# Six instead of four buffers for the down-projection weights, and a later softmax epilogue, in a fused attention and FFN kernel

## The reference

```python
xn = _layernorm(x, axis=-1)
latent = xn @ Wc_down                                  # 1024 -> 512
q = (latent @ Wq_up).reshape(Bsz, Tlen, N_HEAD, HEAD_DIM)
kv = latent @ Wkv_up; k, v = kv[..., :64], kv[..., 64:]
att = softmax(causal(einsum('bthd,bsd->bhts', q, k) * scale))
s = einsum('bhts,bsd->bthd', att, v).reshape(Bsz, Tlen, C) @ Wc_proj
h = _silu(xn @ (w_gate/127).T) * (xn @ (w_up/127).T)
g = _silu(h @ (w_down/127).T)
out = x + s * g
```

## Time and profile before

| | us |
|---|---|
| median of 2 runs | 3336.55 (3332.39 to 3340.7) |
| the profiled execution | 3337.86 |
| its span, slowest core (core 1) | 3336.1 |
| spans of the 8 cores | 3316.5 to 3336.1 |
| mean granted TensorE clock, core 1 | 0.808 |
| ACT busy, core 1 | 1308.0 |
| DVE busy, core 1 | 1181.9 |

### The profile page before, as it was taken

The page is one execution under the profiler, slowest core; times in us unless marked ns, Lnnn a source line. Parts: engine busy times, 40 slices in busy tenths (PEclk is TensorE's granted clock), DMA queues, the critical chain, the costliest instruction groups (busy, mean ns, idle before and its releaser), DMA issues.

```text
span 3336.1 us, 33293 instructions; the slowest of 8 cores (3316.5 to 3336.1 us)
## 1 busy us (share of the span) xinstructions
PE 2123.8 (64%) x10464; PEld 995.9 (30%) x10464; DVE 1181.9 (35%) x1978; ACT 1308.0 (39%) x1457; POOL 417.1 (13%) x329
## 2 busy tenths in 40 slices
PE   2324545466565674785758758587575887587876
PEld 1112323222331341442225222252231442223421
DVE  4635443432533435424243251422322422511221
ACT  0112232312321332433634436344455437376365
POOL 0211221223133011101101001100111001011011
PEclk9556767767787796897879968799788899699997
DMA  5031346759476153351015300153001250011510
GB/s 92 28 65 41 51 79 81 112 92 147 57 87 111 47 123 112 73 137 43 27 46 121 102 15 26 40 134 96 13 20 40 62 147 30 22 27 39 146 39 14
DMA packets 547288, 232.14 MB, mean 70 GB/s; under 512 B 476464, under 2 KB 532784, under 8 KB 547120
## 3 DMA queue, kind: packets, MB, share of 16 engines
q1 hardware_dynamic: 429792, 186.88, 21.5%
q0 software_dynamic: 117328, 43.14, 12.1%
HBM read 241.62 MB, written 27.26 MB: 81 GB/s over the span
## 4 chain that ended last, share of the span: by engine, by line
PE 39%; DVE 20%; DMA 15%; ACT 10%; issue 10%; POOL 4%; DVEq 1%; SPq 0%; ACTq 0%; POOLq 0%
PE ps_sc L566 9%; PE ps_y L553 9%; ACT p_sb L577 9%; PE ps_u L724 5%; PE ps_u L731 4%; POOL p_sb L585 4%; DVE recbf L605 3%; PE ps_u L795 3%; DMA wd_t<-wdbf 3%; DMA wu_t<-wu 3%; DMA xt<-xb 3%; DMA wd_t<-wd 2%; PE ps_u L643 2%; DVE stat L303 2%; DVE xnT L377 2%
## 5 line engine op out<-in xcount | busy, mean ns | idle before, releaser
L577 ACT ACTIVATE p_sb<-ps_sc 128x1024 bf16<-128x1024 f32 x1088 | 1089.1, 1024 | 1460.3 <-PE ps_sc L566 1453.6
L553 PE MATMUL ps_y<-p_sb,vaug_sb 128*65 128x512 bf16 x2176 | 747.4, 429 | 245.6 <-POOL p_sb L585 143.6
L566 PE MATMUL ps_sc<-qs,kT_sb 65*128 65x512 bf16 x2176 | 745.9, 428 | 26.7 <-DVE qs L534 26.7
L585 POOL TENSOR_TENSOR p_sb<-p_sb,masks_sb 128x1024 bf16<-128x1024 bf16 x128 | 277.5, 2177 | 2361.0 <-ACT p_sb L577 2360.7
L553 PEld LDWEIGHTS ps_y<-p_sb,vaug_sb 128*65 128x65 bf16 x2176 | 214.6, 120 | 682.3 <-issue 607.3
L370 PE MATMUL ps_u<-ident_sb,xn_t 128*128 128x128 bf16 x512 | 65.5, 271 | 413.3 <-DVE xn_t L333 236.2
L795 PE MATMUL ps_u<-wd_t,h_sb 128*128 128x512 bf16 x768 | 219.8, 415 | 154.4 <-DMA wd_t<-wd 59.1
L566 PEld LDWEIGHTS ps_sc<-qs,kT_sb 65*128 65x128 bf16 x2176 | 222.0, 107 | 242.8 <-issue 103.1
L724 PE MATMUL ps_u<-xnT_own,wg_t 128*128 128x256 bf16 x1536 | 224.0, 294 | 83.9 <-DVE h_sb L742 60.1
L595 DVE CAST yf<-ps_y 64x1024 bf16<-64x1024 f32 x32 | 38.8, 1213 | 591.3 <-PE ps_y L553 591.3
L731 PE MATMUL ps_u<-xnT_own,wu_t 128*128 128x256 bf16 x1536 | 218.4, 290 | 15.0 <-DMA wu_t<-wu 14.9
(11 more groups left out here) (85 smaller groups left out, 1249.3 us busy)
## 6 DMA issues: line engine op xcount, KB each, us to landing
wg_t<-wgbf SPq DMA_DIRECT2D x144, 256.0 KB, 3.4
wu_t<-wubf SPq DMA_DIRECT2D x144, 256.0 KB, 3.8
wd_t<-wdbf SPq DMA_DIRECT2D x288, 128.0 KB, 2.2
xt<-xb SPq DMA_DIRECT2D x64, 512.0 KB, 4.5
wg_t<-wg POOLq DMA_DIRECT2D x48, 256.0 KB, 7.7
wu_t<-wu POOLq DMA_DIRECT2D x48, 256.0 KB, 8.7
wd_t<-wd POOLq DMA_DIRECT2D x96, 128.0 KB, 4.2
xo_t<-xo SPq DMA_DIRECT2D x16, 512.0 KB, 4.1
```

The source lines that it names most:

```text
L553: last = O("tensor", lambda e_, t=t, nh=nh, par=par: e_.matmul(ps_y[0:65, nh * 512:(nh + 1) * 512], vaug_sb[:, t, :], p_sb[:, par, nh * 51 ...
L566: sct = O("tensor", lambda e_, t=t, nh=nh, sb2=sb2: e_.matmul(ps_sc[:, sb2 * 1024 + nh * 512:sb2 * 1024 + (nh + 1) * 512], kT_sb[0:65, t * ...
L577: ex = O("scalar", lambda e_, sb2=sb2: e_.activation(p_sb[:, sb2, :], ps_sc[:, sb2 * 1024:(sb2 + 1) * 1024], AF.Exp), [sct, st["p_war"][sb ...
L585: mtoks[t] = O("gpsimd", lambda e_, pview=pview, mj=mj: e_.tensor_tensor(pview, pview, masks_sb[:, mj, :].unsqueeze(1).broadcast_to([128, ...
```

## The change

It has two parts. The ring of `wd_t` gets six buffers in place of four, with the loads issued six tiles ahead; six is also the number of tiles in one step. EPI_DELAY goes from 6 to 10 ticks. The write-backs keep their four chains of semaphores (`wb{seq % 4}`).

```diff
--- before.py
+++ after.py
@@ -154,7 +154,7 @@
     wproj_sb = sbuf("wproj_sb", [128, DK, D], BF16)
     wg_t = sbuf("wg_t", [128, 3, DK, 128], BF16)
     wu_t = sbuf("wu_t", [128, 3, DK, 128], BF16)
-    wd_t = sbuf("wd_t", [128, 4, 512], BF16)
+    wd_t = sbuf("wd_t", [128, 6, 512], BF16)
     ident_sb = sbuf("ident_sb", [128, 128], BF16)
     ident2_sb = sbuf("ident2_sb", [128, HD], BF16)
     masks_sb = sbuf("masks_sb", [128, 4, 128], BF16)
@@ -262,7 +262,7 @@
             "xnacc": [None, None],
             "xnT_war": None, "p_war": [None, None], "yT_war": [None, None],
             "o_war": [None, None], "qs_war": None, "hbuf_war": t_teff,
-            "wg_war": [None, None, None], "wu_war": [None, None, None], "wd_war": [None] * 4,
+            "wg_war": [None, None, None], "wu_war": [None, None, None], "wd_war": [None] * 6,
             "vt_war": t_consts, "scbf_war": None, "latq_war": None,
             "ytmp_war": (), "yf_war": None, "rec_war": None,
             "t2_war": None, "u1_war": None, "u2_war": None, "tsb_war": None, "recbf_war": None,
@@ -668,7 +668,7 @@
         wg_wb = {}
         wu_wb = {}
         wd_wb = {}
-        wb_ring = {"g": [None] * 3, "u": [None] * 3, "d": [None] * 4}
+        wb_ring = {"g": [None] * 3, "u": [None] * 3, "d": [None] * 6}
         wb_chain = {}
         proj_emitted = set()
         combine_emitted = set()
@@ -760,7 +760,7 @@
 
             def wd_load(seq):
                 nh_, m_ = divmod(seq, FM)
-                sl_ = seq % 4
+                sl_ = seq % 6
                 src = (wdbf_d if from_bf else wd_d)
                 t = O("sync" if from_bf else "gpsimd",
                       lambda e_, m_=m_, nh_=nh_, sl_=sl_, src=src:
@@ -780,7 +780,7 @@
                 return t
 
             wd_toks = {}
-            for s0 in range(4):
+            for s0 in range(6):
                 wd_toks[s0] = wd_load(s0)
             for nh in range(2):
                 for g4 in range(FM // GM):
@@ -800,8 +800,8 @@
                                 [tdm, h2_toks[m], st["util"] if mi == 0 else None],
                                 out="mm")
                         st["wd_war"][sl_] = dlast
-                        if seq + 4 < 2 * FM:
-                            wd_toks[seq + 4] = wd_load(seq + 4)
+                        if seq + 6 < 2 * FM:
+                            wd_toks[seq + 6] = wd_load(seq + 6)
                     for tc in range(2):
                         eidx, par = accs[tc]
                         dst = o_sb[:, par, nh * 512:(nh + 1) * 512]
@@ -861,7 +861,7 @@
         act_m = [None]
         act_l = [None]
         tick = [0]
-        EPI_DELAY = 6
+        EPI_DELAY = 10
 
         LAZY_STEPS = 1
```

## The result

The changed kernel takes 3239.37 us (median of 11 runs, 3228.48 to 3317.51) against 3339.78 us before (median of 10). The ratio is 0.969 with a 95% interval of 0.966 to 0.972. The forecast was 3225 us with a range of 3193 to 3262 and a chance of 0.89 for faster by over 2%, so it holds, 14 us too low. Executions in which the cores of one die take over 1% longer at a lower clock, as that of 3317.51 us, are left out of the ratios. The profiled execution took 3241.58 us, 96 us less than the one the sum was made against.

What follows compares the result with a forecast made beforehand. No engine is near full, so waits and their order bound the kernel; the ring costs 133 us. Savings of 66 + 11 + 15 + 19 = 111 us from 3337.9 give 3226.9, forecast as 3225 us, range 3193 to 3262.

Steps and rivals of the forecast that it cites:

- The bf16 halves, 66 us: Six halves of eight steps: six buffers recover 66 of 67 us lost to late bf16 loads; step period 4.4 us.
- Slot 9: First down step there: PE's 3.70 us wait goes because tile loads stand ahead of the epilogue's DMA; not counted again.
- Rival 5: No gain, 3338 us: evacuation or ACT takes over each wait; against it, the ninth matmul, never the first, waits. Chance 0.02.
- Half 1, 19 us: Second casting half, 980:1047: 17 us back at 1.02 us a load and share 0.9, plus 2 from the moved epilogue.
- Half 0, 11 + 15 = 26 us: First casting half: all 11 us lost in its first three steps, and 15 of a possible 27 in the other five.
- nothing in these steps is timed by another clock: Bf16 halves: nearly all of the 66 us lies on the path, since PE holds the next scores and ACT idles.
- Part 2 at nothing: Epilogue four ticks later: counted 0 us; L613's wait stays 35 us, gate matmuls meeting the 10.08 us one in slot 2.
- 1, the clock: Casting stretches: PE's clock rises as waits go, 14 us more with all waits gone, 3191 us; chance 0.16.
- 2, casting halves give nothing: Casting halves: descriptors on POOL or write-backs set the pace, so only 66 us come off, 3272 us; chance 0.10.
- 3, half of the bf16 waits stay: Bf16 halves: more loads in flight land over 1.5 us later than 2.85 us, 33 us lost, 3260 us; chance 0.10.
- 4, the epilogue costs by itself: Each of 15 moved epilogues meets a busy DVE and adds a 10.08 us wait, 151 us in all, 3378 us; chance 0.02.

Runs made afterwards that it cites:

- e11_best_epi6: Kernel with eight buffers, split `ps_u` hand-over and early residual loads, but EPI_DELAY 6 instead of 10: ratio interval 0.952 to 0.959, about 11 us slower than with 10.

## Why the prediction was right, and where it was off

**The bf16 halves, 66 us: right.** They measured 67.4 us. The way is the one described: one run of twelve matmuls, a period of 4.29 us where 4.4 was said, 0.67 us left for L813, DMA share 0.57 as worked out. Waits for `wdbf` are 6.2 us where I said under 5. The five-buffer kernel confirms the step timing from the other side.

**Slot 9: the wait of 3.7 us went, as said.** That PE came out of it at the lower clock was not in the sum: with the delay the half gains 5.5 us more than without, not 3.7. It is the delay that removes this wait, since the kernel with six buffers alone still has it, at 3.94 us. Rival 5's "never the first" matmul is not true of this step.

**Half 1, 19 us: right in size (20.4), for a reason that was half right.** I bounded it by a transfer price of 1.02 us a load and a share of 0.9. The share came out at 0.89 in 965:1020, but eight buffers gave 5.5 us more, and half the bytes 11. Landing time and bytes are not two bounds, of which one holds. With 4, 6 and 8 buffers a casting load lands after 4.2, 5.3 and 5.8 us by the medians of the pages' part 6. If all buffers were always loading, that would be 1.05, 0.88 and 0.73 us a load, an estimate: each added buffer gives throughput, and less of it each time.

**Half 0, 11 + 15 = 26 us: nearly right.** It measured 9.1 + 13.2 = 22.3 us. The five steps of the 15 took 56 us on the core that it was read from and now take 41.4 in the mean of the cores, and the share is 0.90 in 722:765, as the prediction has it.

**Ahead of half 0 and behind it: no term, and 2.8 and 7.6 us came back.** The ring's first loads are issued some 65 us ahead of the first down step, and I did not ask what they run beside; the layer norm's waits for `xt` grew by 3.0 us. As to the end, I wrote that nothing in these steps is timed by another clock, and looked no further than the last step. The combine behind them has a load of its own, and that load stands on SP behind write-backs that now wait for each other. 5.5 of the 7.6 us lie at this combine; the other 2.1 lie further on, and their cause is open. That waiting for the residual costs this much is shown by the kernel with early residual loads, which takes back 9.3 us. That the load is late because of the chains of write-backs is read from SP's waits on all cores, and no run with other chains tests it.

**The sum.** The terms of the sum measured 67.4 + 22.3 + 20.4 = 110 us, where 111 were forecast. Against it stand the 7.6 us behind half 0 and the 4.4 ahead of it, and 1.2 us were gained between the other halves, which leaves the table's 99.3. The slowest core gained 96.2 (3336.1 to 3239.9), because it lies 3 us further from the mean of the cores than before. So of the 14 us between forecast and median 8.3 have a place and a cause that the sum lacked, 5.5 at the combine and 2.8 at the layer norm. The rest, with these 3 us in it, is within what one execution differs from another by.

**Part 2 at nothing: 34.7 us at L613 now, 35.5 before, and that is luck.** The wait of 10.1 us in slot 2 has left the row: the gate matmuls meet it now, as I said they would, with 8.79 us at L724 (416.55 us). The wait of 10.9 us behind half 0 has come into it. A sum that stays can hide two changes. The delay alone is worth 0.35% (0.06 to 0.64).

**Rivals.** 1, the clock: it did come back, from 0.62 and 0.86 to 0.79 and 0.90 in the last five steps of half 0 and in half 1, but the casting halves shrank by 42.7 us, not by over 60. 2, casting halves give nothing: out by their stretches, and its mechanism by the half-bytes kernel. 3, half of the bf16 waits stay: out with six buffers, and what five buffers do. 4, the epilogue costs by itself: out, since the delay alone is no slower than before (0.9965). 5, no gain: out by the time.

## What to carry to other kernels

Size a ring by time: a buffer must be free again one landing time before its tile is wanted, and landing time is to be read from the trace under the load that the larger ring makes, not before it. When a stretch is made faster, read what it is handed to: here 7.6 of the 22.3 us that half 0 had gained came back behind it, most of them in waits for a load that was issued at its use, and issuing it earlier gave back 9.3. The first loads of a larger ring collide with what runs where they are issued, here a layer norm (2.8 us). When a ring grows, look also at what else counts in its old size: the write-backs kept four chains for six buffers, and began to wait for each other. When the waits for weights are gone, the hand-over of the accumulator is next; splitting it gave another 1.2%, but only with two more buffers than the step is long; with six it gave 0.4%.

## What was not expected of the hardware

- A casting load costs by its bytes: 1.19 us of the queue's time in a full stretch, 0.60 us with half the bytes and the same number of packets. Before, with gaps, it was 1.02, so the price itself rises somewhat under load. The Trainium skill (DMA: Bandwidth & Descriptors, "Anatomy of one DMA") has the rest of a transfer beside its fixed cost go by bytes; in that the two prices agree with it, but by an estimate from its 436 GB/s the 256 KB that a casting load reads would take 0.6 us, and the measured price is twice that.
- PE restarts at the lower clock after a wait of 3.9 us amid dense work: twelve matmuls took 4.12 us where 2.75 is the rule, 1.4 us on top of the wait. The granted clock is 1.00 in 1790:1799, 0.66 in 1803:1807 and 1.00 in 1807:1812 of that core. After a wait of 7.22 us in `e11_best_epi6` they took 4.09 us. After the wait of 1.34 us in the five-buffer kernel the next two took 0.59 us and the ten of the step behind 2.32, as elsewhere at the upper level.
- Write-backs of 128 KB in half 0 took 4.3 us from issue to landing in place of 2.0 once six casting loads were in flight beside them, and with four chains for six buffers SP waited for them where it had not before.
